# Reordering the opening of a fused attention and mixture-of-experts kernel: weights made inside the first attention, and the first four units laid out by a table

## The reference

```python
# block 0: FiLM-conditioned attention and MLP
h = film(rmsnorm(x, norm1_w), cond, film1_w, film1_b)
Q, K, V = h @ q_w + q_b, h @ k_w + k_b, h @ v_w + v_b
x = x + softmax(Q @ K.T * D ** -0.5) @ V @ proj_w + proj_b
h = film(rmsnorm(x, norm2_w), cond, film2_w, film2_b)
x = x + gelu(h @ mlp_w1 + mlp_b1) @ mlp_w2 + mlp_b2
# block 1: 16 heads of 64, q and k normalised per head, then expert choice
h = _ln(x, ln1_g, ln1_b) + silu(t) @ W_ada.T + b_ada
q, k, v = split(h @ Wqkv.T)
q, k = _ln(q, qn_g, qn_b), _ln(k, kn_g, kn_b)          # over the 64 of a head
x = x + concat(softmax(q @ k.T / 8) @ v) @ Wout.T
gate = softmax(x @ Wgate.T); vals, idx = top_k(gate.T, 128)   # 8 experts
x[idx] += vals * (gelu(_ln(x[idx]) @ fc1.T + b1) @ fc2.T + b2)
```

## Time and profile before

| | us |
|---|---|
| median of 3 runs | 473.28 (472.67 to 474.12) |
| profiled execution | 473.62 |
| its span, first to last instruction | 471.9 |
| PE busy | 419.6 (89%) |
| DVE busy | 303.2 (64%) |
| ACT busy | 299.7 (64%) |
| POOL busy | 186.6 (40%) |
| mean granted TensorE clock | 0.949 of 2.4 GHz |

### The profile page before, as it was taken

How to read it: one execution, slowest core, us unless ns; L and a number is a source line. 1 busy time by engine, 2 the same in 40 slices (tenths; PEclk the granted TensorE clock), 3 DMA queues, 4 the chain that set the end, 5 groups by cost and what they waited for, 6 DMA issues and landing times.

```text
span 471.9 us, 8986 instructions
## 1 busy us (share of the span) xinstructions
PE 419.6 (89%) x2918; PEld 363.0 (77%) x2918; DVE 303.2 (64%) x761; ACT 299.7 (64%) x675; POOL 186.6 (40%) x148
## 2 busy tenths in 40 slices
PE   2998965389999999999999999999998987639996
PEld 1577554269989999999999998999997886528794
DVE  3574365556776776776777677677676437985233
ACT  3255523357878878878887887887886666305631
POOL 5102472734543553553454454355354004235000
PEclk9999997579999999999999999999999997858999
DMA  8300000650000000000000000000000000000001
GB/s 230 106 1 1 1 0 0 193 209 1 1 3 1 1 1 0 0 0 0 0 0 0 0 0 0 0 0 0 0 0 2 1 0 2 0 2 0 1 1 44
DMA packets 7492, 9.49 MB, mean 20 GB/s; under 512 B 371, under 2 KB 4270, under 8 KB 7470
## 3 DMA queue, kind: packets, MB, share of 16 engines
q1 hardware_dynamic: 5646, 7.11, 4.9%
q10 hardware_dynamic: 1824, 2.10, 1.6%
HBM read 8.68 MB, written 0.52 MB: 20 GB/s over the span
## 4 chain that ended last, share of the span: by engine, by line
PE 72%; DVE 5%; issue 1%; ACT 1%; DVEq 0%
PE bank L1255 24%; PE bank L1040 16%; PE pair L1221 9%; PE pair L1240 6%; PE pair L1239 6%; PE bank L1406 2%; PE pair L1040 1%; PE pair L1327 1%; DVE at_least L941 1%; PE pair L1362 1%; PE bank L1362 1%; PE pair L1398 1%; PE pair L1417 1%; PE pair L1379 1%; PE bank L1398 1%
## 5 line engine op out<-in xcount | busy, mean ns | idle before, releaser
L1255 PE MATMUL bank<-v_s,probs_T 128*128 128x128 f32 x1024 | 135.4, 275 | 2.7 <-ACT probs_T L596 1.9
L857 DVE TENSOR_REDUCE negmax<-pair 128x1 f32<-128x512 f32 x128 | 88.1, 688 | 74.8 <-PE pair L1240 74.8
L1255 PEld LDWEIGHTS bank<-v_s,probs_T 128*128 128x128 f32 x1024 | 126.5, 192 | 5.9 <-issue 2.5
L416 POOL TENSOR_TENSOR qk_rstd<-qk_ms,minus_half 128x8 f32<-128x8 f32 x32 | 55.1, 1721 | 132.2 <-DVE qk_ms L828 132.0
L596 ACT ACTIVATE probs_T<-bank 128x512 f32<-128x512 f32 x128 | 76.6, 598 | 44.6 <-PE bank L1040 44.6
L590 ACT ACTIVATE probs<-pair,negmax 128x512 f32<-128x512 f32 x128 | 88.2, 689 | 15.9 <-DVE negmax L857 15.8
L1040 PE MATMUL bank<-ident,probs 128*128 128x128 f32 x512 | 76.6, 272 | 0.0
L1040 PEld LDWEIGHTS bank<-ident,probs 128*128 128x128 f32 x512 | 62.7, 140 | 13.2
L1239 PE MATMUL pair<-k_s,q_s 128*128 128x512 f32 x128 | 61.4, 480 | 0.4 <-ACT probs L590 0.4
L1240 PE MATMUL pair<-k_low,q_s 128*128 128x512 f32 x128 | 50.8, 397 | 0.0
L426 POOL TENSOR_TENSOR q_s<-kq,k_s 64x512 fp32r<-64x512 f32 x32 | 44.0, 1376 | 13.5 <-DVE k_s L843 8.7
(11 more groups left out here) (260 smaller groups left out, 659.5 us busy)
## 6 DMA issues: line engine op xcount, KB each, us to landing
fc_raw<-in_L_cond_fc2s_dram SPq DMA_DIRECT2D x1, 2048.0 KB, 15.2
x_in<-in_x_dram ACTq DMA_DIRECT2D x1, 512.0 KB, 4.7
w<-in_L_cond_mlp_w_dram SPq DMA_DIRECT2D x2, 256.0 KB, 3.2
wout<-in_L_cond_Wout_dram SPq DMA_DIRECT2D x1, 512.0 KB
b_all<-in_L_cond_b2s_dram SPq DMA_DIRECT2D x1, 512.0 KB, 11.5
out_dram<-final SPq DMA_DIRECT2D x2, 256.0 KB, 2.4
film<-in_L_cond_film_w_dram SPq DMA_DIRECT2D x2, 128.0 KB, 5.1
wq<-in_L_cond_q_w_dram SPq DMA_DIRECT2D x1, 64.0 KB, 7.3
```

Source lines behind the costliest of these rows:

```text
L416: pool.tensor_tensor(qk_rstd[:, :, :].rearrange("p c t -> p (c t)"), qk_ms[:, :, :].rearrange("p c t -> p (c t)"), minus_half[:, 0:2 * NC] ...
L857: dve.tensor_reduce(negmax[:, s:s + 1], bank[s % 2][:, :], AX, ALU.max, negate=True)\
L1255: last = pe.matmul(bank[4][:, c * D:c * D + D], probs_T[:, c % 2, k, :], v_s[:, slot, k, :], start=(k == 0), stop=(k == NC - 1))
```

## The change

It does five things.

1. **Weights.** POOL makes a matrix `centring` (identity minus 1/64 within each half), and the q and k weights are multiplied with it in place of being transposed by the identity, which transposes and centres in one product. `w_all`, `wmean` and all that worked on them are gone: ACT copies a bank from PSUM straight into `w_hi`, and DVE subtracts that from the same bank into `w_lo` (`weights_low`), bank by bank. The first six banks all use bank 7 and are made at the end of PE's iterations 1 to 6 of the first attention, the others around `proj0(1)` and behind `down0(0)` in banks 5 and 6.
2. **Batch 0's chain first.** DVE sums the squares of batch 0 before it copies batch 1's attention, and scales batch 0 before `batch_out0(1)`. PE does all `up0` of batch 0, then turns batch 1, then `down0(0)`. The bias mb0 is added per batch. `down0(1)` goes to bank 4 and is done in two halves, around the first two projections. Of batch 0, ACT makes h in two halves and DVE splits it in two; batch 1's centring goes to POOL, and its norm, transposes, h (now on ACT) and split are moved into unit 0 of the second attention.
3. **Pieces 0 and 1.** DVE does their two subtractions (`lows_here`), ACT the copy of q and the last copy of k (`q_high`, `k_low_beside`); piece 1 has another tile for its input (`kq_from`). The tables of ACT are loaded at other places.
4. **Later pieces.** Only pieces 0 and 1 are projected before the first unit. In the first four units the steps of pieces 2 to 7 stand where a table `OPENING` says, each as (unit, chunk): piece; from the fifth unit on the loop is as before. Piece 3's subtractions are on DVE.
5. **SP** waits for the third split of h before the experts' loads.

The core of the diff:

```diff
+        OPENING = dict(turn={(1, 0): 2, (1, 2): 3, (2, 2): 4, (3, 1): 5},
+                       project={(0, 3): 2, (1, 0): 3, (1, 3): 4, (2, 2): 5, (3, 1): 6, (3, 3): 7},
+                       enter={(1, 0): 2, (1, 1): 3, (2, 0): 4, (2, 3): 5, (3, 2): 6},
+                       affine={(1, 1): 2, (1, 3): 3, (2, 3): 4, (3, 2): 5},
+                       place={(1, 1): 2, (1, 3): 3, (2, 3): 4, (3, 3): 5},
+                       total={(0, 3): 2, (1, 1): 3, (2, 0): 4, (2, 3): 5, (3, 2): 6},
+                       norm={(0, 3): 2, (1, 2): 3, (2, 1): 4, (3, 0): 5, (3, 3): 6},
+                       high={(1, 1): 2, (1, 3): 3, (2, 3): 4, (3, 2): 5},
+                       low={(1, 3): 2, (3, 0): 4, (3, 3): 5})
...
             sp.wait_ge(qkv_done, 1)
-            sp.wait_ge(h_split, 2)
-            sp.wait_ge(w_split, 3)
+            sp.wait_ge(h_split, 3)
+            sp.wait_ge(wT_copied, W_BANKS + 1)
...
+            link(pool.memset(centring[:, :], 0.0))
+            link(pool.memset(centring[0:HD, 0:HD], -1.0 / HD))
+            link(pool.memset(centring[HD:P, HD:P], -1.0 / HD))
+            pool.tensor_tensor(centring[:, :], centring[:, :], ident[:, :], ALU.add).then_inc(centring_ready, 1)
...
             piece_scale(0, 0)
             piece_scale(1, 0)
-            piece_low(0, 0, 2)
-            piece_low(1, 1, 2)
+            at = slice(NC, TC)
+            pool.wait_ge(centre_ready, 1)
+            pool.tensor_tensor(xn[:, at, :], x_att[:, at, :], spread(centre[:, at], [P, NC, D]), ALU.add)\
+                .then_inc(norm_in, 1)
+            norm_scale(2, 1, EPS1)
             piece_scale(2, 2)
-            body(0)
+            piece_scale(3, 2)
+            piece_low(2, 2, 4)
+            piece_scale(4, 4)
+            for p in (4, 5):
+                piece_scale(p + 1, p)
+                piece_low(p, p, p + 2)
...
             for g in range(TC):
                 act.wait_ge(max0_done, g + 1)
...
                 if g >= 2:
                     turned0(g - 2)
+                if 1 <= g <= QK_BANKS + WOUT_BANKS:
+                    copy_weights(g - 1)
...
             piece_in(0, 0)
             piece_in(1, 1)
+            piece_place(0, 0)
+            piece_place(1, 1)
             piece_affine(0)
-            piece_place(0, 0)
+            q_high(0)
             piece_affine(1)
-            piece_in(2, 2)
-            piece_place(1, 1)
+            act.wait_ge(norm_in, 2)
+            square(xn, 1)
+            k_low_beside(0)
+            q_high(1)
+            k_low_beside(1)
...
+            def weights_low(n):
+
+                dve.wait_ge(wT_copied, n + 1)
+                dve.tensor_tensor(weight_part(w_lo, n), weight_psum(n), weight_part(w_hi, n).bitcast(F32),
+                                  ALU.subtract).then_inc(w_split, 1)
...
+                if 2 <= g <= QK_BANKS + 1:
+                    weights_low(g - 2)
                 if g == 2:
                     late_cols()
...
+            for n in range(QK_BANKS + WOUT_BANKS + 2, W_BANKS):
+                weights_low(n)
...
-                        if c == 0 and not (last and j >= PER - 3):
-                            piece_ss(u + 3)
-                        if c == 1 and not (last and j >= PER - 2):
-                            piece_high(u + 2, j + 2)
-                        if c == 2 and not (last and j >= PER - 3):
-                            piece_norm(u + 3, j + 3)
+                        if start and c == 0:
+                            scaled(2, 1, xn)
+                        if start and c == 1:
+                            dve.wait_ge(h_act, 5)
+                            split_h(N, TOK)
+                        if first and j == 1 and c == 3:
+                            piece_low(2, 2)
+                        if not (last and j >= PER - 2):
+                            for p, p_in in due("high", first, u, j, c, 1, 2):
+                                piece_high(p, p_in)
+                        if not (last and j >= PER - 3):
+                            for p, _ in due("total", first, u, j, c, 0, 3):
+                                piece_ss(p)
+                        if not (last and j >= PER - 3):
+                            for p, p_in in due("norm", first, u, j, c, 2, 3):
+                                piece_norm(p, p_in)
+                        if first and j == 1 and c == 3:
+                            lows_here(3)
+                            piece_low(3, 3)
...
+            def make_weights(n):
+                dst = weight_bank(n)
+                if n == 0:
+                    pe.wait_ge(wqkv_in, 16)
+                    pe.wait_ge(v0_ready, 1)
+                    pe.wait_ge(centring_ready, 1)
+                elif n <= QK_BANKS + WOUT_BANKS:
+                    pe.wait_ge(wT_copied, n)
+                    pe.wait_ge(w_split, min(n, QK_BANKS))
...
+                if 1 <= g <= QK_BANKS + WOUT_BANKS:
+                    make_weights(g - 1)
...
             project(0, 0, 0)
+            pe.wait_ge(h_split, 2)
             project(1, 1, 0)
-            turn_norm(2, 1)
+            down0(1, range(NC // 2, NC))
             turn_piece(0, 0)
             turn_piece(1, 1)
-            pe.wait_ge(h_split, 2)
-            project(2, 2, 0)
-            project(3, 3, 0)
             body(0, first=True)
```

More of the change, by code:

```diff
@@ L160, in film_attention_then_expert_choice @@
         loop = Area(max(early.at, experts.at))
-        wqkv_raw = Area(loop.at)("wqkv_raw", [P, WC, D])
         w_start = loop.at
@@ L890, in _ @@
+                        if first and j == 1 and c == 3:
+                            lows_here(3)
+                            piece_low(3, 3)
+                        elif not (last and j >= PER - 2):
+                            for p, p_in in due("low", first, u, j, c, 3, 2):
+                                piece_low(p, p_in)
             piece_ss(0)
-            scaled(2, 1, xn)
+            dve.wait_ge(ss_done, 1)
+            piece_ss(1)
             piece_norm(0, 0)
-            piece_ss(1)
```

318 lines of the change are left out of this document (171 added, 147 removed).

## The result

| | before | after |
|---|---|---|
| median, us | 473.70 (472.67 to 474.38) | 484.53 (483.48 to 485.27, 4 runs) |
| ratio | | 1.0229, interval 1.0199 to 1.0258 |
| profiled execution | 473.62 | 483.48 |
| its span | 471.9 | 481.7 |

A forecast was written before the change was run, and what follows sets the result against it. PE was taken as the bound from unit 1 on, so only unit 4's first score mattered: opening to 84.0, then units with 16.5 us of waits to 139.0, 5.8 later than before; 473.3 + 5.8 = 479 us, range 469 to 484.

The forecast's parts named there:

- Step 1: First attention: weight banks wait for DVE's subtraction, last score at 38.6 instead of 33.0, 5.6 us lost (bounds 2.6 to 7).
- the four matmuls 0.44: First attention: PE time to make one weight bank with the centring matrix, taken as 0.44 us.
- Step 2: From the first attention to batch 0's h: project(0) at 69.9 us instead of 74.71, 4.8 us gained.
- the charge of 0.7: Before down0(0): DVE's product slowed beside POOL's mb0 addition, 0.7 us, bounds 0 and 1.2.
- Step 3: Pieces 0 and 1, up to the second attention: first score at 84.0 us instead of 98.28, 14.3 us won.
- the 0.5 for POOL's centring: Pieces 0 and 1: POOL's centring of batch 1 beside high(0) adds 0.5 us (0 to 1.2).
- Step 4: Units 0 to 3, second attention: PE waits for piece chains, 16.5 us; unit 4 at 139.0, 5.8 us later than 133.17.
- my 38.1: Units 0 to 3, second attention: they would take 38.1 us if PE never waited, against 34.89 today.
- the 55.0: Units 0 to 3, second attention: their forecast duration with PE's waits, 55.0 us.
- rival 3: Units 0 and 1: waits could keep the clock at 1.2 GHz through both; 483 us, chance 0.15.
- Rival 1: Units 2 and 3: their 7.7 us of waits don't arise, unit 4 at 131.3; 471.3 us, chance 0.25.
- Rival 2: First attention: `weights_low` doesn't hold PE, costing 2.6 instead of 5.6 us; 474 us, chance 0.10.

The follow-up runs named there:

- e3: Changed kernel with the q and k weight banks made in banks 7 and 6 in turn instead of 7 alone; 480.06 us, ratio 1.0119.
- e2: Changed kernel with q and k weights transposed by the identity instead of multiplied by the centring matrix; 482.92 us, ratio 1.0193.
- e10: Changed kernel with POOL adding mb0 for batch 0 before, not after, its scale of batch 1's second norm; 484.98 us, ratio 1.0221.
- e1: Changed kernel with filler transposes on PE in four waits of units 0 to 3; 481.59 us, ratio 1.0146.
- e5: Changed kernel with a rearranged table for units 0 to 3, POOL also subtracting piece 2 before scaling piece 3; 471.55 us, ratio 0.9951.
- e12: The changed kernel run again, unaltered; 484.92 us, ratio 1.0213 against the kernel before.
- e9: Changed kernel with both the filler transposes of e1 and the identity transposes of e2; 478.81 us, ratio 1.0090.
- e6: e5 together with the two weight banks of e3; 468.11 us, ratio 0.9880.
- e8: Kernel before, with only the subtractions and copies of pieces 0 and 1 moved to DVE and ACT; 471.69 us, ratio 0.9946.
- e7: Changed kernel with its new opening, but units 0 to 3 in the order of the kernel before; 473.26 us, ratio 0.9990.
- e11: e6 with the POOL order of e10; 467.67 us, ratio 0.9875.

## Why the prediction was right in direction and too small

Both kernels' time was read from one event, unit 4's first score. That held: it moved by 10.9 us and the median by 10.8.

**Step 1, the first attention.** The mechanism is right. PE waits for `weights_low` at the places named, and e3, which takes that away, gains 4.15 us up to the last score. The failed term is the bank's own cost, "the four matmuls 0.44": a product of f32 by the centring matrix takes 0.97 us where the transposes take 0.46. My sentence that multiplying "costs what the transposes cost" is wrong. I took 0.44 as a fifth of an iteration, because score and mix "each stream twice the columns" of the transposes. They don't. The timeline of the kernel before has the transposes and the mix over the same four times 128 columns:

```profile
31.67 0.60 PE L1040 MATMUL bank<-ident,p 128*128 128x128 f32 x4
32.11 1.06 PE L1115 MATMUL bank<-pT,v 128*128 128x128 f32 x8
```

From start to start the transposes take 0.44 us and the mix, a product like that by `centring`, 0.89 (the next score is at 33.00). The price was there to be read. With transposes (e2) the last score comes 19.72 us behind the first, my 19.7; as written, 21.50. In e2 the single terms hold as well: against the kernel before iterations 2 to 6 lose 2.26, 0.28, 1.29, 1.32 and 0.44 us, for a forecast of 2.3, 0.2, 1.35, 1.35 and 0.44.

**Step 2.** Between the last score and project(0) I had 31.3 us (69.9 - 38.6), and the profile has 31.3 (52.84 - 21.50). To that tenth it is luck. The first `up0` starts 11.7 us behind the last score (51.55 - 39.89) for a forecast of 10.8, and `block_out(0)` 23.15 (63.04 - 39.89) for 23.1, so errors of nearly 1 us cancelled. The product beside POOL's add lost 1.06 (1.75 - 0.69) and not 0.7, but all except 0.16 of that lay beside the Gelus (e10), so the charge of 0.7 stood for something that costs the path next to nothing.

**Step 3.** Project(0) to the first score was forecast at 14.1 us and took 13.8 (66.63 - 52.84). Of the 0.5 for POOL's centring beside the high copy 0.2 was seen: the cast took 0.65 us, against 0.43 for that of piece 1. Together the first score came at 85.0 for 84.0, and by the measure of the table 1.5 us late (66.63 for 84.0 - 18.87 = 65.1): 1.8 of step 1 less the 0.3 of this step.

**Step 4.** The waits, as forecast and as measured: turn(2) 3.2 and 3.04; turn(3) 3.45 and 3.14; unit 2's scores 2.1 and 2.06; turn(4) 0.75 and none, for PE came late to it at half clock (in e1 there is one of 0.54); turn(5) 2.4 and 1.28; project(7) 4.3 and 3.87. That is 16.2 us forecast and 13.4 measured. Against it the units hold more PE work than my 38.1 (39.46 us busy in e5) and some 1.6 us of short waits that I didn't have, so that the 55.0 fits e1's 55.24 in part by luck. The order in the queues was the right cause, and e5 shows it: moving the same steps takes 12 us away. What failed is that rival 3's clock was kept out of the forecast as another case. It is no alternative to the waits but comes behind them, and not in units 0 and 1 alone, as I had written, but behind the waits of units 1, 2 and 3. Units 0 to 3 took 59.0 us (60.1 in e12) for my 55.0, and with the clock held (e1) 55.2. So 3.8 to 4.9 us are the clock's, a term that the sum had for unit 0's start and put at nothing for the waits behind it.

1.5 and 4.0 us are 5.5 of the 5.6 us between the forecast 5.8 and the 11.4 of the table (125.67 - 114.30). With both taken out (e9) the median is 478.81, where 479 was forecast; its six runs lie between 476.36 and 481.92, so this confirms the two terms together only roughly.

**The rivals.** Rival 1 falls: the waits of units 2 and 3 are there. That the opening pays if the units wait less is true of e5 and e6, which needed another order for it. Rival 2 falls by e3. Rival 3's 483 was nearest, with its place too narrow; it should have had more of the chance. The Trainium skill, page TensorE: Matmul & The Clock Gate, section "What's actually happening", has the halved clock as the state that activity releases. The 0.57 behind the waits agrees with that, and so does the 1.00 of e1, where transposes fill them.

**What the change is worth in its parts.** The subtractions of pieces 0 and 1 on DVE gain 0.5% (e8). The whole opening, these included, gains nothing while the units stay as they were (e7), so the rest of it loses what e8 gains. With the units rearranged it gains 12.8 us at the first score, and the arrangement given loses all of that and 11 us more. With a better table (e5) the kernel ends 0.5% below the kernel before, and with a second bank for the weights too (e6, e11) 1.2%.

## What to carry to other kernels

An opening that hands its work to the loop behind it is worth only what that loop can hide; before moving a step, write down for each engine's queue when its inputs are ready in the new place, POOL's queue and the reuse of each single tile with it. Waits of the matmul engine in a stretch that runs at 2.4 GHz can cost more than themselves: here 13.4 us of them in four units brought 3.8 to 4.9 us of slowed matmuls. Price a product from a row of the same operation and type, since a transposing row of the same size took half here (0.44 for 0.89 us).

## What the runs showed of the hardware that I had not expected

- A product of f32 operands over 4 x 128 columns holds PE for 0.89 us in eight records (0.96 to 0.97 behind a wait), the same columns transposed by the identity for 0.44 in four (0.46 behind a wait). The Trainium skill, page FP8 and Floating Point Precision, section "TensorE Precision Notes", says that a true f32 product takes four passes. An estimate from that is 0.92 us, four times the 0.23 us from start to start of an fp32r product of 512 columns in the changed kernel (98.45 to 98.68), if that is one pass; the 0.89 agrees with it.
- Behind the same wait of 3.04 us the granted clock stayed at 1.00 in one execution of the changed kernel (transposes 0.66 us) and fell in another (1.12 us, 0.68 in the window). Behind the waits before turn(3) (3.14 and 3.15 us), unit 2 (2.06 and 2.10) and project(7) (3.87 and 3.88) it fell both times, about 1 us later than the end of the wait in the case of unit 2. Behind the 1.28 us before turn(5) it stayed. In e5 no wait inside the units exceeded 1.82 us, and it stayed at 1.00 from 100 to 142 us.
- DVE's product of two SBUF tiles took 1.75 us beside a POOL add of 1.26 us, and ended 0.55 us behind it; without it it took 0.69. On the path that cost 0.16 us at most, since the Gelus ended as late. The Trainium skill, page SBUF — State Buffer, section "SBUF: two separate sides", has the common port pair held for a whole instruction, with the other engine blocked. The rows agree with that to 0.15 us: product, cast of step 3 and the product of the kernel before in the earlier trace rows end 0.55, 0.28 and 0.54 us behind POOL's instruction, and alone they take 0.69, 0.43 and 0.69.
- The start of the first attention varies by 2 us between executions (17.91 to 19.93), against medians of the kernel before that lie within 0.5 us of each other (473.70 to 474.15). A comparison of two profiles is sharper when counted from there.
